# Second attention: scores and key lengths from the features themselves, without projecting the keys

## The reference, cut to what matters

```
features_n = rmsnorm(features, fn_w)                    # 4 x 1601 x 512
Q = einsum('btd,fd->btf', text, Wq_w) + Wq_b            # text = layernorm(x)
K = einsum('bsd,fd->bsf', features_n, Wk_w) + Wk_b
Q = rmsnorm(Q, qn_w)
K = rmsnorm(K, kn_w)
attn = softmax(einsum('btf,bsf->bts', Q, K) / sqrt(512))
attended = einsum('bts,bsf->btf', attn, features_n)     # the unprojected features are the values
x = x + attended
```

## Time and profile before

| | us |
|---|---|
| median of 3 runs (3175.95 to 3185.04) | 3179.64 |
| the profiled execution | 3190.52 |
| its span, first to last instruction | 3188.8 |
| PE busy | 3040.3 |
| DVE busy | 2104.0 |
| ACT busy | 1733.4 |
| POOL busy | 908.0 |

### The profile page before, as it was taken

The page is one execution under the profiler, slowest core; times in us unless marked ns, Lnnn a source line. Parts: engine busy times, 40 slices in busy tenths (PEclk is TensorE's granted clock), DMA queues, the critical chain, the costliest instruction groups (busy, mean ns, idle before and its releaser), DMA issues. The chain is left out here.

```text
span 3188.8 us, 54146 instructions
## 1 busy us (share of the span) xinstructions
PE 3040.3 (95%) x18566; PEld 2702.9 (85%) x18566; DVE 2104.0 (66%) x3215; ACT 1733.4 (54%) x3277; POOL 908.0 (28%) x742
## 2 busy tenths in 40 slices
PE   8999998999999999999999999979989799998897
PEld 7888887899999999899998999968768788886786
DVE  4433343788888888788887888854454567766675
ACT  4433344676666666666666666642243344443472
POOL 0000121344444444444444444432200124440101
PEclk9999999999999999999999999999989799999998
DMA  7665696766777776677766777557540111111683
GB/s 253 216 214 200 207 289 200 152 159 161 165 160 158 163 157 164 150 165 158 160 160 155 160 158 163 127 148 238 190 160 32 57 29 41 41 41 30 236 289 129
DMA packets 375894, 497.03 MB, mean 156 GB/s; under 512 B 34316, under 2 KB 283452, under 8 KB 375640
## 3 DMA queue, kind: packets, MB, share of 16 engines
q1 hardware_dynamic: 373080, 485.40, 56.8%
q0 software_dynamic: 2560, 8.39, 0.8%
HBM read 225.57 MB, written 133.87 MB: 113 GB/s over the span
## 5 line engine op out<-in xcount | busy, mean ns | idle before, releaser
L725 POOL TENSOR_TENSOR a_t_lo<-a_turned,a_t_hi 128x512 fp32r<-128x512 f32 x512 | 649.7, 1291 | 937.9 <-ACT a_t_hi L854 937.9
L845 ACT ACTIVATE a_probs<-a_ps_s,a_neg_max 128x1024 f32<-128x1024 f32 (+1 forms) x512 | 529.2, 1034 | 474.7 <-DVE a_neg_max L897 468.8
L890 DVE TENSOR_REDUCE a_half_max<-a_ps_s 128x1 f32<-128x1024 f32 (+1 forms) x512 | 571.1, 1115 | 190.9 <-PE a_ps_s L742 186.7
L740 PE MATMUL a_ps_s<-a_k_buf,a_q_buf 128*128 128x512 f32 (+1 forms) x1024 | 420.1, 410 | 17.9 <-ACT a_probs L845 11.9
L741 PE MATMUL a_ps_s<-a_k_buf,a_q_buf 128*128 128x512 f32 (+1 forms) x1024 | 385.7, 377 | 0.0
L742 PE MATMUL a_ps_s<-a_k_buf,a_q_buf 128*128 128x512 f32 (+1 forms) x1024 | 384.8, 376 | 0.0
L926 DVE TENSOR_TENSOR a_x_lo<-a_ps_x,a_x_hi 128x512 fp32r<-128x512 f32 (+1 forms) x512 | 314.3, 614 | 106.6 <-ACT a_x_hi L863 106.6
L916 DVE STREAM_TRANSPOSE a_turned<-xn 128x512 f32<-128x512 f32 x512 | 357.4, 698 | 0.0
L472 DVE TENSOR_TENSOR p_out<-p_ps_j,p_out 128x512 fp32r<-128x512 f32 (+3 forms) x196 | 153.3, 782 | 302.4 <-ACT p_out L400 302.4
L400 ACT ACTIVATE p_out<-p_ps_j 128x512 fp32r<-128x512 f32 (+3 forms) x196 | 141.9, 724 | 311.4 <-PE p_ps_j L293 311.4
L740 PE MATMUL a_ps_o<-a_t_hi,a_v_buf 128*128 128x256 f32 x1024 | 298.8, 292 | 6.1 <-issue 3.6
(11 more groups left out here) (394 smaller groups left out, 7102.0 us busy)
## 6 DMA issues: line engine op xcount, KB each, us to landing
xn<-a_probs SPq DMA_DIRECT2D x1024, 128.0 KB, 3.4
a_q_all<-p_out SPq DMA_DIRECT2D x64, 512.0 KB
a_q_buf<-a_q_all SPq DMA_DIRECT2D x128, 256.0 KB, 3.2
a_k_buf<-a_k_all SPq DMA_DIRECT2D x64, 464.5 KB, 4.0
a_v_all<-p_out SPq DMA_DIRECT2D x56, 512.0 KB
a_k_all<-p_out SPq DMA_DIRECT2D x48, 384.0 KB
a_v_buf<-a_v_all SPq DMA_DIRECT2D x64, 256.0 KB
a_o_all<-a_o_part SPq DMA_DIRECT2D x128, 128.0 KB, 3.1
```

The source lines that it names most:

```text
L725: pool.tensor_tensor(t_lo[:, slot, :, :], turned[:, slot, :, :], t_hi[:, slot, :, :].bitcast(F32), ALU.subtract).then_inc(t_done, 1)
L740: pe.matmul(o, w_hi, m_hi, start=first, stop=False)
L845: act.activation(probs[j][u.a][:, lo:hi], s_flat[:, lo:hi], ACT.Exp, bias=neg_max[:, j:j + 1], scale=SCALE, accum_out=half_sum[:, bass.ds( ...
L890: dve.reduce_max(half_max[:, half:half + 1], s_flat[:, lo:hi], AX.X).then_inc(max_done, 1)
```

## The change

The keys are no longer projected. With W = Wk times fn_w by columns, the length of the key of a feature row r is r G r + 2 u r + |bk|^2, where G = W'W and u = W'bk. G and u are made once. G is symmetric, so only its upper triangle is kept, with the part right of the diagonal block doubled; for each context tile the product of the tile with the triangle has 512, 384, 256 and 128 columns for the four chunks, and the linear term 2u is added to the same bank by one product whose stationary operand is two rows of ones and whose moving operand is 2u, split in a high and a low row. DVE multiplies the bank by the tile and sums along the row. The queries instead go through the keys' weights once for all batches (`through_keys`), and the scores are products of these with the turned features. The constant that bk adds to each score comes from `query_sums`.

With this the preparation changes: the norm of x is no block of its own any more, the keys' weights, the vectors and the row of fn_w are loaded during the experts' block (and scaled there by POOL), and the key products, the second product of the queries and longer query sums are added. In the loop, scaling a tile and its high part move from DVE and POOL to ACT, the ring has six buffers, the first tile of the next batch is turned ahead of the end of this one, and the inverses of the key lengths are computed on rows and spread by 13 plain products with a pattern of ones (`spread_inverses`). The scores, the softmax and the weighing stay, in a slightly different order.

```diff
@@ gated_experts_block, sync
+            sp.dma_start(key_w_rows[:, :, :], key_w.rearrange("(t p) d -> p t d", p=P)).then_inc(key_loaded, 16)
...
             sp.dma_start(slot_rows, zeros[:, :].unsqueeze(1).to_broadcast([P, slot_rows.shape[1], D])).then_inc(cleared, 16)
@@ gated_experts_block, gpsimd
+            for f in range(DC):
+                pool.tensor_tensor(key_w_rows[:, f, :], key_w_rows[:, f, :], fn_row[:, :], ALU.mult).then_inc(key_scaled, 1)
@@ normed_attention_block
-    RING = 4
+    RING = 6
-        norm_block(nc, held, x_res, xn, stats, 1e-5, "norm2", prefetch=load_weights)
@@ gpsimd
+            for f in range(DC):
+                pool.wait_ge(w1_hi_done, f + 1)
+                pool.tensor_tensor(w1_lo[:, f, :], key_w[:, f, :], w1_hi[:, f, :].bitcast(F32), ALU.subtract).then_inc(w1_done, 1)
@@ tensor, before the loop
+            def key_product(f):
+                pe.wait_ge(w1_done, f + 1)
+                for c in range(DC):
+                    mm = three(ps_s[:, c, c * P:D], w1_hi[:, f, c * P:(c + 1) * P], w1_lo[:, f, c * P:(c + 1) * P],
+                               w1_hi[:, f, c * P:D], w1_lo[:, f, c * P:D], f == 0, f == DC - 1)
+            def key_bias():
+                for f in range(DC):
+                    mm = pe.matmul(ps_p[:, 0, :], bk_wide[:, f, :], key_w[:, f, :], start=f == 0, stop=f == DC - 1)
...
+                for f in range(DC):
+                    mm = pe.matmul(ps_p[:, 1, D - 1:D], bk_wide[:, f, :], columns[:, BK, f:f + 1], start=f == 0, stop=f == DC - 1)
+            def through_keys(i):
...
+                for c in range(DC):
...
+                    for f in range(DC):
+                        mm = three(ps_s[:, 2 + c % 2, 0:TOK], w2_hi[:, f, c * P:(c + 1) * P], w2_lo[:, f, c * P:(c + 1) * P],
+                                   qt_hi[i % 2][:, f, :], qt_lo[i % 2][:, f, :], f == 0, f == DC - 1)
+            def query_sums(i):
...
+                for j in range(QT):
+                    at = QT * i + j
+                    for f in range(DC):
+                        pe.matmul(ps_p[:, 0, at:at + 1], squared[i % 2][:, f, j * P:(j + 1) * P], ones[:, 0:1],
+                                  start=f == 0, stop=f == DC - 1)
+                    for f in range(DC):
+                        pe.matmul(ps_p[:, 1, at:at + 1], qt_hi[i % 2][:, f, j * P:(j + 1) * P].bitcast(F32), z_col[:, f:f + 1],
+                                  start=f == 0, stop=False)
+                        mm = pe.matmul(ps_p[:, 1, at:at + 1], qt_lo[i % 2][:, f, j * P:(j + 1) * P].bitcast(F32), z_col[:, f:f + 1],
+                                       start=False, stop=f == DC - 1)
...
             for i in range(B):
                 if i + 1 < B:
                     transpose_x(i + 1)
+                project(i)
                 if i:
-                    sum_query_squares(i - 1)
+                    through_keys(i - 1)
+                    query_sums(i - 1)
@@ tensor, in the loop
-                        project(f, s % 2, COLS[s][1]).then_inc(kp_ps, 1)
+                def key_products(t):
+                    n = rows_of(t)
+                    pe.wait_ge(ft_done, KT * b + t + 1)
...
+                    if t >= 4:
+                        pe.wait_ge(sum_kept, KT * b + t - 3)
+                    pe.matmul(ps_s[0:n, t % 4, :], one_pair[:, 0:n], u_pair[:, :], start=True, stop=False)
+                    for c in range(DC):
+                        m_hi, m_lo = (g[:, g_at[c]:g_at[c] + D - c * P] for g in (g_hi, g_lo))
+                        mm = three(ps_s[0:n, t % 4, c * P:D], k_hi[:, c, t * P:t * P + n], k_lo[:, c, t * P:t * P + n],
+                                   m_hi, m_lo, False, c == DC - 1)
...
+                for t in range(KT):
...
+                        transpose_features(t + 1, KT * b)
+                    key_products(t)
@@ scalar, in the loop
+                for t in range(KT):
...
+                        scale_tile(b, t + 2)
...
+                        features_hi(b, t + 1)
...
+                    act.activation(f_hi[0:n, t, :], raw[0:n, t % RING, :], ACT.Copy).then_inc(f_hi_done, 1)
@@ vector, in the loop
+                    dve.scalar_tensor_tensor(held_at[0:n, :], ps_s[0:n, t % 4, :], 1.0, raw[0:n, t % RING, :], ALU.mult, ALU.mult,
+                                             accum_out=key_sum[0:n, t:t + 1]).then_inc(sum_kept, 1)
```

More of the change, by code:

```diff
@@ L1445, in normed_attention_block @@
[L1445 to L1453, removed]
+        g_at = [D * c - P * (c * (c - 1) // 2) for c in range(DC)]
@@ new lines, in _, with scores @@
+                    key_products(t)
+                    if t == FIRST + 1:
+                        turn_norms(0)
+                spread_inverses(0)
+                def scores(j, ch):
+                    c0, n = CHUNKS[ch]
+                    if j:
+                        pe.wait_ge(s_scaled, PRIMED + 2 * QT * b + ch // 2 + 1)
+                    else:
+                        pe.wait_ge(sum_kept, KT * b + max(t for t in range(KT) if t % 4 == ch) + 1)
+                    for c in range(DC):
+                        mm = three(ps_s[:, ch, 0:n], q_hi[:, c, j * P:(j + 1) * P], q_lo[:, c, j * P:(j + 1) * P],
+                                   k_hi[:, c, c0:c0 + n], k_lo[:, c, c0:c0 + n], c == 0, c == DC - 1)
+                    return mm
@@ L1721, in _ @@
                     inputs_hi(i + 1)
+                if i == 0:
+                    for f in range(DC):
+                        act.activation(w2_hi[:, f, :], key_w[:, f, :], ACT.Copy, scale=qk_w[:, f:f + 1]).then_inc(w2_hi_done, 1)
                 for f in range(DC):
@@ L1728, in _ @@
+                if i == B - 2:
+                    act.wait_ge(c_inv, 1)
+                    scale_tile(0, 0)
+                    scale_tile(0, 1)
+            features_hi(0, 0)
             act.wait_ge(qs_ps, B)
-            act.activation(q_inv[:, :], ps_p[:, 0, 0:TILES], ACT.Sqrt, bias=eps_col[:, :], scale=1.0 / D).then_inc(q_root, 1)
-            act.activation(inverse[:, :], ctx_squares[:, :], ACT.Sqrt, bias=eps_col[:, :], scale=1.0 / D).then_inc(c_root, 1)
-            for c in range(DC):
-                weights_hi(DC + c)
+            act.activation(q_root[:, :], ps_p[:, 0, 0:TILES], ACT.Sqrt, bias=eps_col[:, :], scale=1.0 / D).then_inc(root_done, 1)
@@ new lines, in _, with exponents @@
+                key_inverses(0)
+                key_inverses(1)
+                key_roots(1)
+                key_inverses(2)
+                key_inverses(3)
+                def exponents(j):
+                    act.wait_ge(neg_max_done, QT * b + j + 1)
+                    for half, (lo, hi) in enumerate(HALVES):
+                        act.activation(probs[j][:, lo:hi], probs[j][:, lo:hi], ACT.Exp, bias=neg_max[:, j:j + 1], scale=q_now[:, SC, j:j + 1],
+                                       accum_out=half_sum[:, j, half:half + 1]).then_inc(probs_done, 1)
@@ new lines, in features_lo @@
+            def features_lo(place, t):
+                n = rows_of(t)
+                dve.wait_ge(ft_hi_done, KT * place + t + 1)
+                dve.tensor_tensor(k_lo[:, :, t * P:t * P + n], by_chunk(ps_t[:, t % 2, :], n),
+                                  k_hi[:, :, t * P:t * P + n].bitcast(F32), ALU.subtract).then_inc(ft_done, 1)
+            for t in range(TILES):
+                dve.bn_aggr(mean_var[:, t, :], stats[:, t, :]).then_inc(mean_done, 1)
+            dve.wait_ge(mean_done, TILES)
@@ new lines, in _ @@
+            dve.wait_ge(bk_ps, 1)
+            dve.tensor_copy(bk_square[:, :], ps_p[:, 1, D - 1:D]).then_inc(bk_done, 1)
+            weights_lo(2)
+            for c in range(DC):
+                dve.wait_ge(g_hi_done, sum(len(g_parts(a)) for a in range(c + 1)))
+                for at, n, scale in g_parts(c):
+                    to = g_at[c] + at - c * P
+                    dve.scalar_tensor_tensor(g_lo[:, to:to + n], ps_s[:, c, at:at + n], scale, g_hi[:, to:to + n].bitcast(F32),
+                                             ALU.mult, ALU.subtract).then_inc(g_done, 1)
@@ L1945, in _ @@
-                output(b, 1)
+                for t in range(KT):
+                    if t + 1 < KT:
+                        features_lo(b, t + 1)
+                    key_sum_of(t)
+                    if t == FIRST - 1:
+                        key_norms(0)
+                    if t == KT - 2:
+                        invert(0)
+                key_norms(1)
+                dve.wait_ge(now_done, b + 1)
+                scale_scores(0, 0)
+                invert(1)
+                scale_scores(0, 1)
```

691 lines of the change are left out of this document (388 added, 303 removed).

## The result

The changed kernel takes **3204.2 us** (median of 4 runs, 3199.8 to 3205.6) against 3179.2 (median of 4, 3176.0 to 3185.0): ratio **1.0076, 95% interval 1.0063 to 1.0088**. It is 25 us slower. That is the upper end of the predicted range, 3168 to 3204; the likeliest case was no change, 3184.

The account below looks back on a forecast made before the run. PE was taken to bound the batches. Preparation +55.0 and loop -50.5 gave +4.5 us, which on the median 3179.6 made 3184 us, no change; range 3168 to 3204.

Parts of the forecast that it names:

- One two-row product (0.23): Loop, each of 13 tiles per batch: the linear term's product priced at 0.23 us within a tile of 2.58.
- The rest of the loop: Four batches: 36.9 us replaces 48.0 of keys in each, batches of 82.2; loop -50.5 us in all.
- the waits in the softmax: Loop, each batch: PE's 3.2 us wait for the softmax stays, about 0.3 shorter.
- The first rival: Last 128-column products of tiles and key products, 168 in all, cost 0.215 us each: 17.6 us more, 3202; chance 0.22.
- a floor for each product: Split-type products of 128 columns: 0.11 us taken, since 66 columns cost the same 0.11 as one column.
- The third rival: Loop: ACT falls behind and PE waits; 0.3 us per tile beyond its slack would be 16 us, 3200; chance 0.09.
- The preparation: Stage before the batches: 85.3 PE work, 3.9 start, 7.5 waits, 16.6 clock; 113.3 us against 58.3, +55.0.
- The waits: Preparation, about 7.5 us: some 3 after the last key product, 0.8 at first x tiles, some 3.7 over sixteen query banks.
- the two further rises of the clock: Preparation: at the first key product and after the 3 us wait, each costing 1.7 us.
- the experts' block would hide the new loads and multiplications: Experts' stage of 158.2 us: key weights' load, scaling and later clearing of slots costed at nothing.
- The clock in the sums: Preparation, four sums of 48 records: each loses 1.6 us at half clock and 1.7 behind it, 13.2 in all.
- the second rival: Preparation: the clock stays up through the four sums, so 13.2 us fall away, 3171; chance 0.14.

Follow-up runs that it names:

- the full-row run: Changed kernel with the linear term's product taking 128 rows instead of 64 (rows of ones and 2u at 0 and 64, rest zeros): 3184.8 us, ratio 1.0019.
- the kernel with the constant by a row: Changed kernel with 128 rows for the linear term and the long query sums replaced by one row made once: 3165.1 us, ratio 0.9952.

## Where the prediction held and where it failed, by its own steps

- **"One two-row product (0.23)" is the step that failed.** The product itself costs 0.23 (with full rows against none: 2.56 - 2.32 = 0.24), but with 64 rows it adds about 0.38 for the two changes of height. A tile was priced at 2.58 and took 2.94. Over 52 tiles 0.38 comes to 20 us, and the full-row run gives back 19.4. The price was taken by the columns; the rows were not asked about, though the experts' block of the same trace had a one-row product to read.
- **The rest of the loop held in sum.** With that product mended it takes 332.4 against 332.1 forecast. That it is so close is luck, because single terms were off both ways. Products of 128 columns were cheaper (0.28 for three, not 0.33), and the waits in the softmax were 1.7 and 0.3, not 2.9. Against that, the clock fell four times in that run's loop, each for 3.4 us, and its first 4.9 us ran at the half clock that the last sum leaves, which the prediction had put into the preparation.
- **The first rival, short products charged by the column, is refuted:** the three start 0.06 and 0.11 apart (2599.96, 2600.02, 2600.13), not 0.21. The prediction called 0.11 a floor for each product; it isn't one. With weights of 65 columns, in the last tile, all three start 0.06 apart (2603.75, 2603.81, 2603.87 in the kernel with the constant by a row), so 0.11 goes with weights of 128 columns. The Trainium skill, TensorE: Matmul & The Clock Gate (Back-to-back issue gap), gives about 56 ns for an isolated product of 128 columns, without its weight load. The 0.06 agrees with it; the 0.11 between products with 128-column weights doesn't.
- **The third rival, ACT behind in the loop, is refuted.** No tile waits for ACT; the second batch's keys have PE busy for 39.55 of 39.90 us, and without the linear term tiles come even 2.32 apart.
- **The preparation:** 108.7 for 113.3. The first key product came 4.1 us in (3.9 forecast). The waits were 1.7, 0.8 and 1.9, together 4.4, where 7.5 was priced: 1.7 for 3 behind the last key product, and 1.9 for 3.7 in the query banks, of which only two waited. Of the two further rises of the clock only the first came in this profile: from 2488.8 to 2529.6 the granted clock was 1.00. That the experts' block would hide the new loads and multiplications held: 157.6 us, 158.2 before.
- **The clock in the sums was right:** the four took 6.3, 6.8, 6.6 and 7.5, together 27.2, against 21.7 + 4 x 1.6 = 28.1 forecast, and what ran behind them was at half clock for 3.6 to 5.6 us each. Spreading the products gave 13.3 us, forecast 13.2. So the second rival, "the clock holds through the sums", is refuted.
- **The range and the chances:** two large terms of opposite sign came as forecast, but 50.4 - 30.2 leaves 20 us and not 4.5. What moved the result from no change to slower was the one instruction that is added 52 times, priced by analogy and given no rival of its own. The range reached as far as 3204 for the first and third rivals, and neither came; that the time is at its end and not far outside is luck.

## What to carry to other kernels

Read a small matmul's price from a row of its own height, not only of its width. Among products of 128 rows, one of 64 rows cost 0.4 us more here and a run of products of 8 or 5 rows 0.3 or 0.2, while 65 rows with zeros in them cost nothing extra, so pad the rows. Spread long runs of one-column products among others, or replace them by one row made once. With that row and with all rows padded, this change runs in 3155 us instead of 3204, 0.8% under the kernel before.

## What had not been expected of the hardware

- No weight load overlaps the product before it at a change between 64 rows and 128: the loads stand idle for 0.17 and 0.24 us with nothing to wait for, and a tile grows from 2.56 to 2.94 us. With 65 rows tiles are 2.56 us apart.
- Sixteen records of products of 8 rows (2.0 us) were followed by 3.4 us at the granted clock 0.50, though PE was busy throughout; of the eight runs of 8 or 5 rows in a loop two to five were. With 65 or 128 rows, zeros in all but 8 or 5, the clock stayed at 1.00 through the whole loop of 321 us.
- Three products of 128 columns in the split type start 0.06 and 0.11 us apart with weights of 128 columns, and 0.06 and 0.06 with weights of 65.
